# An expert feed-forward layer on one core: the up products in fp32 as 64x64 tiles, without their hi/lo splits

## The reference, cut to what matters

```python
# x: (32 sequences, 64 tokens, 1024); itok: one of 16 ids for each sequence
# layer 0: c = x @ adapter[id].T ; x1 = x + c @ W_base.T + bias + LoRA part (top 2 of 8 experts)
x = x + L0_ffn(L0_cond(x, ...))
# layer 1
y = einsum('bct,bcd->bdt', x, mix[id])        # mixes the 64 tokens of a sequence
t = y.reshape(2048, 1024)[:, perm]            # 16 heads of 64 features
t = einsum('bhd,hdm->bhm', t, up)             # up:   64 -> 256 for each head
t = gelu(t, approximate=False)
t = einsum('bhm,hmd->bhd', t, down)           # down: 256 -> 64 for each head
x = x + t[:, unperm]
```

## Time and profile before

| | |
|---|---|
| median of 3 runs | 620.41 us (619.83 to 621.81) |
| the profiled execution, its own time | 619.76 us |
| its span, first to last instruction | 617.7 us |
| TensorE busy | 598.6 us (97%) |
| VectorE busy | 440.4 us (71%) |
| ScalarE busy | 139.3 us (23%) |
| GpSimd busy | 127.6 us (21%) |
| mean granted TensorE clock | 0.995 of full speed |

### The profile page before, as it was taken

The page is one execution under the profiler, slowest core; times in us unless marked ns, Lnnn a source line. Parts: engine busy times, 40 slices in busy tenths (PEclk is TensorE's granted clock), DMA queues, the critical chain, the costliest instruction groups (busy, mean ns, idle before and its releaser), DMA issues.

```text
span 617.7 us, 13527 instructions
## 1 busy us (share of the span) xinstructions
PE 598.6 (97%) x4439; PEld 348.3 (56%) x4440; DVE 440.4 (71%) x1232; ACT 139.3 (23%) x269; POOL 127.6 (21%) x194
## 2 busy tenths in 40 slices
PE   4899999999999999999999999999999999999996
PEld 3343444444444444447667676767676767676762
DVE  3056666666666666698878897879987889887862
ACT  3001000000000000153314432325342335232333
POOL 4100000111111110060013131313131313131313
PEclk9899999999999999999999999999999999999999
DMA  8998798998899988011023232223132223222222
GB/s 262 399 407 304 268 295 300 310 301 293 305 401 404 385 297 298 22 49 46 10 62 98 65 95 68 87 65 97 59 96 67 88 64 96 68 85 68 85 62 93
DMA packets 43425, 106.89 MB, mean 173 GB/s; under 512 B 8450, under 2 KB 17666, under 8 KB 43394
## 3 DMA queue, kind: packets, MB, share of 16 engines
q1 hardware_dynamic: 31202, 76.57, 36.1%
q0 software_dynamic: 6784, 21.51, 10.4%
q10 hardware_dynamic: 5408, 8.43, 4.1%
HBM read 98.09 MB, written 8.39 MB: 172 GB/s over the span
## 4 chain that ended last, share of the span: by engine, by line
PE 93%; DVE 3%; DMA 1%; issue 1%; SPq 0%; DVEq 0%; POOL 0%; POOLq 0%
PE wide L515 33%; PE bank L618 19%; PE bank L626 9%; PE bank L698 8%; PE wide L681 8%; PE y_wide L546 5%; PE y_wide L661 3%; PE wide L530 2%; PE bank L638 1%; PE bank L639 1%; PE bank L642 1%; DMA ring<-adapters_dram 1%; PE bank L710 1%; DVE c_lo L1149 1%; PE bank L554 0%
## 5 line engine op out<-in xcount | busy, mean ns | idle before, releaser
L515 PE MATMUL wide<-ring,x_in 128*64 128x512 f32 x960 | 209.3, 593 | 0.0
L1198 DVE STREAM_TRANSPOSE x_tok<-xres 32x128 f32<-32x128 f32 x480 | 145.1, 302 | 6.3
L1040 DVE STREAM_TRANSPOSE c_pair<-wide 32x256 f32<-32x256 f32 x240 | 107.1, 446 | 50.4 <-PE wide L515 24.9
L515 PEld LDWEIGHTS wide<-ring,x_in 128*64 128x64 f32 x960 | 68.1, 137 | 128.2 <-issue 128.0
L894 ACT ACTIVATE act_sb<-wide 128x512 f32<-128x512 f32 x120 | 66.5, 610 | 192.9 <-PE wide L681 192.9
L618 PE MATMUL bank<-c_hi,base_t 128*128 128x512 f32 x384 | 102.3, 390 | 0.0
L407 POOL DMA_INDIRECT xres<-xT_dram,row_in x32 | 35.4, 1105 | 232.7 <-DVE out_sb L1189 229.4
L618 PEld LDWEIGHTS bank<-c_hi,base_t 128*128 128x128 f32 x384 | 72.0, 188 | 15.4
L626 PE MATMUL bank<-c_lo,base_t 128*128 (+1 forms) x256 | 78.2, 391 | 0.1
L445 POOL COPY c_all<-c_pair 128x512 f32 x30 | 19.3, 670 | 199.5 <-DVE c_pair L1040 199.5
L698 PE MATMUL wide<-act_sb,down_sb 64*64 64x512 f32 x224 | 54.4, 602 | 0.0
(11 more groups left out here) (150 smaller groups left out, 574.2 us busy)
## 6 DMA issues: line engine op xcount, KB each, us to landing
ring<-adapters_dram SPq DMA_DIRECT2D x128, 512.0 KB, 6.1
x_in<-x_seq_dram ACTq DMA_DIRECT2D x30, 256.0 KB, 4.8
up_raw<-up_dram SPq DMA_DIRECT2D x64, 64.0 KB, 2.3
down_sb<-down_dram SPq DMA_DIRECT2D x32, 128.0 KB, 2.3
ar_sb<-lora_a_router_dram ACTq DMA_DIRECT2D x1, 544.0 KB, 4.3
x_in<-x_seq_dram SPq DMA_DIRECT2D x2, 256.0 KB, 4.3
mix_sb<-mix_dram SPq DMA_DIRECT2D x32, 16.0 KB, 2.0
xres<-xT_dram,row_in POOLq DMA_INDIRECT x32, 3.5
```

The source lines that it names most:

```text
L515: last = pe.matmul(acc[half][h][z * TOK:(z + 1) * TOK, :], x_in[:, half, z, k, :], ring[:, k, z, h * HALF:(h + 1) * HALF], start=(k == 0), ...
L1040: last = nc.vector.transpose(c_pair[r * SQ:(r + 1) * SQ, :, q * SQ:(q + 1) * SQ], wide[half][q * SQ:(q + 1) * SQ, :, :] .rearrange("p h (k ...
L1198: last = nc.vector.transpose(x1_tok[q * SQ:(q + 1) * SQ, :].rearrange("p (c f) -> p c f", f=P)[:, :, f * SQ:(f + 1) * SQ], xres[f * SQ:(f ...
```

## The change

Up is computed in fp32, as down and mix already are, in two quads of 64x64 products a block: for each m the two column halves c of the hidden part and the two heads. So up_hi, up_lo, y_hi and y_lo go, with the functions that made them; y is copied once out of PSUM (`y_kept`), and up's weights lie in two buffers which SyncE fills alternately. `up_begun` is a semaphore that TensorE only increments. The order of VectorE and ScalarE is otherwise as it was.

```diff
 
         act_last = at(weights_at, "act_last", [P, 4, GT])
         x1_last = at(weights_at + 8192, "x1_last", [P, GT])
-        y_hi_last = at(weights_at + 10240, "y_hi_last", [P, GT], F32R)
-        y_lo_last = at(weights_at + 12288, "y_lo_last", [P, GT], F32R)
+        y_last = at(weights_at + 10240, "y_last", [P, GT])
         x_in_at = region(8)
         x_in = at(x_in_at, "x_in", [P, 2, 2, KT, TOK])
-        up_raw = at(x_in_at, "up_raw", [P, HIDDEN])
-        up_hi = at(x_in_at + 2048, "up_hi", [P, HIDDEN], F32R)
-        up_lo = at(x_in_at + 4096, "up_lo", [P, HIDDEN], F32R)
+        up_sb = at(x_in_at, "up_sb", [P, 2, HIDDEN])
         down_sb = at(x_in_at + 6144, "down_sb", [P, 2, 2, 2, HD])
         c_tok_at = region(8)
         c_tok = at(c_tok_at, "c_tok", [P, D])
...
 
             return last_d_ps if late(g, j, 1) else d_ps
 
-        def y_split(g, j):
-
-            return (y_hi_last, y_lo_last) if late(g, j, 1) else (y_hi, y_lo)
+        def y_of(g, j):
+
+            return y_last if late(g, j, 1) else y_sb
 
         def c_hi_of(g, part):
 
...
             def load_up(j):
 
                 for head in range(2):
-                    sp.dma_start(up_raw[head * HD:(head + 1) * HD, :],
-                                 up[:, (2 * j + head) * HIDDEN:(2 * j + head + 1) * HIDDEN]).then_inc(up_in, 16)
+                    sp.dma_start(up_sb[head * HD:(head + 1) * HD, j % 2, :],
+                                 up[:, (2 * j + head) * HIDDEN:(2 * j + head + 1) * HIDDEN]).then_inc(up_in[j % 2], 16)
 
             def load_down(j):
                 sp.dma_start(down_sb[:, j % 2, :, :, :], down[:, 2 * j:2 * j + 2, :, :]).then_inc(down_in[j % 2], 16)
...
             def step(g, j):
 
                 g1, j1 = g + (j + 1) // STEPS, (j + 1) % STEPS
-                sp.wait_ge(up_ok, g * STEPS + j + 1)
+                sp.wait_ge(u_done, (g * STEPS + j) * 2)
                 load_up(j1)
                 if 2 <= j < 2 + GP and not (isinstance(g, int) and g == GROUPS - 1):
                     if j == 2:
...
                 sp.wait_ge(d_done, g * STEPS + j)
                 load_down(j1)
 
-            sp.wait_ge(up_ok, 1)
             load_up(1)
             with sp.Fori(0, GROUPS - 1) as g:
                 for j in range(1, STEPS + 1):
...
 
             def up_heads(g, j):
 
-                pe.wait_ge(up_hi_ok, g * STEPS + j + 1)
-                pe.wait_ge(y_hi_ok, g * STEPS + j + 1)
-                y_hi, y_lo = y_split(g, j)
+                pe.wait_ge(up_in[j % 2], (g * (STEPS // 2) + j // 2 + 1) * 32)
+                pe.wait_ge(y_ok, g * STEPS + j + 1)
+                y = y_of(g, j)
                 for m in range(2):
+                    if not early(g, j, 1):
+                        pe.wait_ge(act_ok, (g * STEPS + j) * 4 - 2 + 2 * m)
                     if m == 1 and not early(g, j, 1) and not late(g, j, 3):
                         pe.wait_ge(half_kept, g * STEPS + j)
-                    for n, (w, y) in enumerate(((up_hi, y_hi), (up_lo, y_hi), (up_hi, y_lo))):
-                        if m == 0 and n == 1:
-                            pe.wait_ge(up_ok, g * STEPS + j + 1)
-                        if m == 0 and n == 2:
-                            pe.wait_ge(y_ok, g * STEPS + j + 1)
+                    pe.sem_inc(up_begun, 1)
+                    for c in range(2):
                         for head in range(2):
                             rows = slice(head * HD, (head + 1) * HD)
-                            last = pe.matmul(u_ps[2 * m + head][:, :], w[rows, m * P:(m + 1) * P], y[rows, :],
-                                             start=(n == 0), stop=(n == 2))
+                            last = pe.matmul(u_ps[2 * m + head][c * HD:(c + 1) * HD, :],
+                                             up_sb[rows, j % 2, m * P + c * HD:m * P + (c + 1) * HD], y[rows, :],
+                                             start=True, stop=True, skip_group_check=True)
                     last.then_inc(u_done, 1)
 
             def down_halves(g, j):
...
                 act.wait_ge(tr_done, way + 1)
                 nc.scalar.copy(x1_tok[:, :], ps[:, :]).then_inc(x1_tok_ok, 1)
 
-            def up_leading(g, j):
-
-                act.wait_ge(up_in, (g * STEPS + j) * 32 + 32)
-                nc.scalar.copy(up_hi[:, :], up_raw[:, :]).then_inc(up_hi_ok, 1)
-
-            def y_leading(g, j):
+            def y_kept(g, j):
                 act.wait_ge(y_done, g * STEPS + j + 1)
-                nc.scalar.copy(y_split(g, j)[0][:, :].rearrange("f (p z t) -> f p z t", z=2, t=TOK), y_ps)                     .then_inc(y_hi_ok, 1)
+                nc.scalar.copy(y_of(g, j)[:, :].rearrange("f (p z t) -> f p z t", z=2, t=TOK), y_ps).then_inc(y_ok, 1)
 
             def mix_here(g):
 
...
                 gelu(g2, j2, 0)
                 gelu(g2, j2, 1)
                 if late(g, j, 1):
-                    y_leading(g1, j1)
+                    y_kept(g1, j1)
                     x1_tokens(1, x1_last, last_d_ps)
                 gelu(g2, j2, 2)
                 if not late(g, j, 1):
-                    y_leading(g1, j1)
+                    y_kept(g1, j1)
                 if j == 0:
                     mix_here(g)
                 gelu(g2, j2, 3)
-                up_leading(g1, j1)
                 if j == 5 and not late(g, j, STEPS):
                     hw_leading(g + 1)
                     act.wait_ge(base_ok, KT)
                     c_leading(g + 1, 0)
 
             over_steps(act, step)
-            y_leading(GROUPS - 1, STEPS - 1)
+            y_kept(GROUPS - 1, STEPS - 1)
             for i in range(4):
                 gelu(GROUPS - 1, STEPS - 2, i)
-            up_leading(GROUPS - 1, STEPS - 1)
             for i in range(4):
                 gelu(GROUPS - 1, STEPS - 1, i)
 
...
                 nc.vector.scalar_tensor_tensor(out=xres[:, b, :], in0=c_bank(g, j)[:, :], scalar=bias[:, j:j + 1],
                                                in1=xres[:, b, :], op0=ALU.add, op1=ALU.add).then_inc(x1_ok, 1)
 
-            def up_rest(g, j):
-                dve.wait_ge(up_hi_ok, g * STEPS + j + 1)
-                nc.vector.tensor_tensor(up_lo[:, :], up_raw[:, :], up_hi[:, :].bitcast(F32),
-                                        ALU.subtract).then_inc(up_ok, 1)
-
-            def y_rest(g, j):
-                dve.wait_ge(y_hi_ok, g * STEPS + j + 1)
-                y_hi, y_lo = y_split(g, j)
-                nc.vector.tensor_tensor(y_lo[:, :].rearrange("f (p z t) -> f p z t", z=2, t=TOK), y_ps,
-                                        y_hi[:, :].bitcast(F32).rearrange("f (p z t) -> f p z t", z=2, t=TOK),
-                                        ALU.subtract).then_inc(y_ok, 1)
-
             def result(g, j):
 
 
...
                     c_rest(g + 1, 1)
                 layer0_out(g, j)
                 if early(g, j, 2):
-                    up_rest(g1, j1)
-                    y_rest(g1, j1)
                     x1_turned(g, j)
                     return
                 if late(g, j, 1):
-                    y_rest(g1, j1)
-                    up_rest(g1, j1)
                     result(g3, j3)
                     return
                 if j == STEPS - 1:
                     result(g3, j3)
                     c_rest(g + 1, 2)
                     c_rest(g + 1, 3)
-                    y_rest(g1, j1)
                     x1_turned(g, j)
-                    up_rest(g1, j1)
                     return
                 if not early(g, j, 3):
                     result(g3, j3)
                 x1_turned(g, j)
-                up_rest(g1, j1)
-                y_rest(g1, j1)
                 if early(g, j, 4):
                     base_rest(SPLIT_ORDER[j + 4])
                 if j == 5 and not late(g, j, STEPS):
```

More of the change, by code:

```diff
@@ L139, in build @@
         ar_sb = at(ar_at, "ar_sb", [P, KT, AR])
-        y_hi = at(ar_at, "y_hi", [P, GT], F32R)
-        y_lo = at(ar_at + 2048, "y_lo", [P, GT], F32R)
+        y_sb = at(ar_at, "y_sb", [P, GT])
         hw_at, b_at = region(8), region(4)
@@ L191, in build @@
         half_ps = banks[3]
-        ids_in, sort_ids_in, perm_in, ar_in, b_in, bias_in, mix_in, up_in = (
-            sem(n) for n in ("ids_in", "sort_ids_in", "perm_in", "ar_in", "b_in", "bias_in", "mix_in", "up_in"))
+        ids_in, sort_ids_in, perm_in, ar_in, b_in, bias_in, mix_in = (
+            sem(n) for n in ("ids_in", "sort_ids_in", "perm_in", "ar_in", "b_in", "bias_in", "mix_in"))
+        up_in = [sem(f"up_in{i}") for i in range(2)]
+        up_begun = sem("up_begun")
         base_in = [sem(f"base_in{j}") for j in range(KT)]
@@ L214, in build @@
             sem(n) for n in ("router_done", "gap_ok", "tanh_ok", "chain", "hw_ok", "hw_tr_done", "hw_t_ok"))
[L215 to L218, removed]
+        part_used, c_hi_ok, c_lo_ok, hw_hi_ok, hw_lo_ok = (
+            sem(n) for n in ("part_used", "c_hi_ok", "c_lo_ok", "hw_hi_ok", "hw_lo_ok"))
+        c_done, x1_ok, tr_done, x1_tok_ok, y_done, y_ok = (
```

(4 more changed lines are left out.)

## The result

The changed kernel takes 628.15 us (median of 4 runs, 627.72 to 629.30) against 620.69 (4 runs): a ratio of 1.0122, 95% interval 1.010 to 1.0144. It is slower by 7.5 us where 17.6 less was forecast, and outside the range of 598.0 to 606.5. In the profiled executions the span went from 617.7 to 625.7, 8.0 us.

What follows compares the result with a forecast made beforehand. TensorE's queue was taken to bound every step, 10.28 us. Savings of 13.4 + 1.5 + 1.2 + 1.5 = 17.6 us off the profiled 619.76 give 602.2; with the median 0.65 above, 602.8 us, range 598.0 to 606.5.

Steps and rivals of the forecast that it cites:

- What bounds the kernel: Whole step: TensorE's queue, start to start, sets the time; PE is busy for all 10.28 us.
- What a quad costs: Down's fp32 quads stand 0.43 us apart, the first 0.48; a change of tile shape adds a drain of 0.09.
- point 1: Up's products: 12 in six pairs become 8 in two quads, saving 0.73 us a step without any wait.
- quads 0.8 apart: Up in the changed kernel's profile: quads standing this far apart would show the forecast wrong; about 0.65 was expected.
- The rule against it: Up's fp32 quads: four passes make each 0.91 us, total 626.6 us; put within a 0.05 chance.
- Point 2: Up's m = 1 waits until 2.90 us after Td, the step's first down start; 0.48 saved, 13.4 over 28 blocks.
- Point 3: Up of blocks 0 and 29, without the wait in front of other work: 2 x 0.73 = 1.5 us saved.
- Point 4: Third step: the transposes its mix waits for end sooner, so mix starts 1.2 us sooner.
- Point 5: The end, from mix 31: shorter up blocks, with no late wait for gelus, save 1.5 us.
- Point 6, 8, 9: VectorE and ScalarE lose work without saving time; SyncE's DMAs and GpSimd's x rows cost nothing, with 2 us left.
- Point 7: Up's new `act_ok` waits and the two semaphore increments in TensorE's queue: cost nothing.
- The rival on the slow side: Up's column halves share moving rows and go in turn, a quad taking 0.86: 623.4 us, chance 0.05.

Runs made afterwards that it cites:

- e5: Changed kernel with up's waits moved ahead of down and every up product on 256 of its 512 token columns: 605.43 us, ratio 0.9760.
- e4: Kernel before the change, with VectorE making the transposes ahead of y's low part in its second step: 619.61 us, ratio 0.9987.
- e3: Changed kernel with up's waits except `half_kept`, and one of two semaphore increments, moved ahead of down: 624.53 us, ratio 1.0064.
- e1: Changed kernel with the second column half of each hidden half left out of up, 4 products instead of 8: 626.61 us, ratio 1.0102.
- e2: Changed kernel with up as 64x128 fp32 products, two a hidden half, instead of four of 64x64: 629.98 us, ratio 1.0168.
- e6: Changed kernel, waits left in place, with every up product on 256 of its 512 token columns: 603.68 us, ratio 0.9735.

## Why the prediction was wrong, point by point

- **What bounds the kernel**: right, before and after. PE's queue, start to start, gives every step.
- **What a quad costs, the step that failed.** "The three quads of down ... stand 1.29 / 3 = 0.43 apart" is what the rows say, but a row is an instruction, and point 1 multiplied it by the products of the code ("12 in six pairs become 8 in two quads"). Down has 8 products in the code and 16 instructions in the trace, and so would up. The text ahead of the prediction carries the same slip in its "16 products" of down and "32" of mix: these are instructions. Right is 0.86 for a quad of fp32 products, four rounds for up's two quads. With that figure in the prediction's own sum, base would start at 2.25 + 4 x 0.43 + 0.09 = Td + 4.06 instead of 3.93: 0.13 more a step, not 0.73 less. Measured ahead of the loop: 4.09, as the drain behind up is 0.13 or 0.14 here, 0.16 more a step. The prediction's own sign of being wrong, quads 0.8 apart, is what the profile shows: 0.88 in the step shown (491.78 and 492.66).
- **The rule against it.** The Trainium skill, "FP8 and Floating Point Precision", section "TensorE Precision Notes", says that true fp32 takes four passes. The runs agree: 0.86 for 512 columns, four times 0.215. The prediction set it aside by comparing the four passes of a product with the time of an instruction, which is half a product; it gave the rule 0.05 where the counts on the profile's page had already decided for it. The price worked out from it, 626.6, is 1.5 us from the result, but by luck: it took slots of 0.23 for the passes, 0.23 a step for the products where 0.15 was measured (2.6 us too much), and had nothing for the loop's gap (4.0 too little).
- **Point 2, the wait for `half_kept`.** Right as a mechanism and never reached: m = 1 comes 0.86 behind m = 0, at Td + 3.3 in the step shown (491.78 + 0.86 = 492.64), 0.5 after the release. e5 shows it with its forecast size: m = 1 at Td + 2.95 in the loop and + 2.86 ahead of it, where 2.90 was forecast. "The add can't come sooner, its start hangs on `d_done`" is not the whole of it: the same `d_done` lets it start 0.1 sooner outside the loop.
- **Point 3 and the sum.** Blocks with no wait were to save 0.73; all 32 cost 0.15 or 0.16 more for their products, some 4.8 us.
- **Point 4, the third step.** 1.2 forecast, 1.15 measured (7.13 to 5.98). e4 gets a third of it with another order of the same work.
- **Point 5, the end.** 1.5 less forecast, 0.4 more measured: two blocks of up with four rounds each instead of the two that were counted. None of the waits that it worked through was late.
- **Point 6, 8, 9.** VectorE, SyncE and GpSimd cost nothing, as said.
- **Point 7, "the two semaphore increments ... nothing".** Wrong in the loop, as a set with the waits: 0.07 to 0.24 behind mix in 24 steps, 3.6 us by e3. The prediction took its evidence from mix's own increment, which stands behind the four long rounds of down, where the queue has time.
- **The ledger.** 4.8 for products, 4.0 for the loop (24 x 0.17, 0.14 of it the gap behind mix and 0.03 within up), 1.15 less in the third step, 0.27 by chance ahead of mix 0: 7.9 of the 8.0.
- **The rival on the slow side** had the quad at 0.86 and 623.4 us, but from column halves that go in turn. e1 refutes that mechanism; the number comes near e3's 624.53, which has only the price of the products, because a quad's true price is the same.

## What to carry to other kernels

Before a duration in the trace is multiplied by a count from the code, divide the group's xcount by the calls in the code: here 16 for 8, and the whole forecast hung on that factor of two. On these rows an fp32 product costs 0.86 us for 512 columns, however much of the array its corners fill, and one in fp32r 0.23, so here three fp32r products for hi and lo parts (0.69) cost less than one in fp32, as the work of splitting lay beside TensorE's and not in its way. Put waits and semaphore instructions of a loop behind long products, not behind a burst of short ones: here that was worth 3.6 us.

## What the runs showed that was not expected

- Each wait, increment or register instruction in TensorE's queue behind mix's 64 short instructions takes 0.10 to 0.16 us. Two of them cost nothing, three cost 0.07 to 0.10 a step and four 0.17 to 0.24 (0.46 everywhere with the waits moved, e3). Behind a change of tile shape most of that disappears (e2: 0.57 and 0.63 to 0.68, with 0.57 outside the loop).
- VectorE's first add starts 0.1 later behind down in the loop (Td + 2.11) than outside it (2.01 or 2.02), in the kernel before, the changed one, e5 and e6 alike. Why was not tried.
- The drain from 64x64 fp32 tiles to 128x128 products is 0.13 to 0.14 with the waits in the changed kernel (1.86 less 4 x 0.43) and 0.11 in e3 (1.83), against 0.09 from 64x128 fp32r. Why they differ is open.
- Filling two corners of the array or four takes the same time for the same columns (e1), also where the products share their moving rows.
